# A fused Mamba and RWKV layer: the residual by accumulating transposes, a norm's factor on VectorE, another order of the stages

## What is computed

```python
x = x + mamba(layernorm(x))          # ends in its own norm over y @ W_out + its input
x = x + rwkv_channel_mix(layernorm(x))

# mamba(xn), D = 256 channels, N = 16 states
x, z = split(xn @ W_in)
delta = softplus((x @ W_x)[:, :D] @ W_dt + b_dt)
B, C  = the other 2 * 16 columns of x @ W_x
h_t   = exp(delta_t * A) * h_(t-1) + delta_t * x_t * B_t     # for each channel and state
y_t   = sum over the 16 states of h_t * C_t, + x_t * D_param
res   = (y * silu(z)) @ W_out + xn
out   = norm(res) * ln_g + ln_b

# rwkv_channel_mix(h): r = sigmoid(mix_r @ W_r.T); k = relu(mix_k @ W_k.T) ** 2; out = r * (k @ W_v.T)
```

## Time and profile before

| | |
|---|---|
| three runs | 1000.49, 996.27 and 998.63 us, median 998.63 |
| the profiled execution | 995.58 us, span 993.7 us |
| PE, DVE, ACT, POOL busy | 94%, 92%, 92%, 94% of the span |
| mean granted clock | 0.983 of full speed |
| instructions of POOL on 128x1024 | 255 of dbx (L519), 144 of the C product (L532) |
| HBM | 164 GB/s over the span |

### The profile page before, as it was taken

How to read it: one execution, slowest core, us unless ns; L and a number is a source line. 1 busy time by engine, 2 the same in 40 slices (tenths; PEclk the granted TensorE clock), 3 DMA queues, 4 the chain that set the end, 5 groups by cost and what they waited for, 6 DMA issues and landing times.

```text
span 993.7 us, 15849 instructions
## 1 busy us (share of the span) xinstructions
PE 934.1 (94%) x5040; PEld 720.7 (73%) x5040; DVE 913.4 (92%) x1005; ACT 912.2 (92%) x2154; POOL 932.8 (94%) x409
## 2 busy tenths in 40 slices
PE   8757779999999999999999999999999999999997
PEld 5345566877868687786868778686877878688876
DVE  2899998999999999999999999999999999999875
...
GB/s 209 166 164 178 151 212 192 149 192 165 201 150 210 214 149 193 163 198 153 203 222 146 198 152 205 158 195 215 147 208 142 202 170 192 189 146 206 119 75 22
DMA packets 51473, 171.99 MB, mean 173 GB/s; under 512 B 5440, under 2 KB 32576, under 8 KB 35008
## 3 DMA queue, kind: packets, MB, share of 16 engines
...
...
HBM read 153.67 MB, written 9.44 MB: 164 GB/s over the span
## 4 chain that ended last, share of the span: by engine, by line
PE 45%; ACT 36%; DVE 8%; issue 7%; POOL 2%; DMA 1%; SPq 0%; DVEq 0%; ACTq 0%; POOLq 0%
PE w_ps L1249 12%; ACT da_ps L632 11%; PE y_ps L1233 10%; PE w_ps L1242 9%; DVE da_ps L986 3%; ACT xn_tok L572 3%; DVE hg L986 3%; PE w_ps L1314 2%; ACT spare L578 2%; PE w_ps L1371 2%; PE w_ps L1355 2%; ACT L782 2%; ACT L773 2%; ACT zs L773 1%; ACT r_out L779 1%
## 5 line engine op out<-in xcount | busy, mean ns | idle before, releaser
L519 POOL TENSOR_TENSOR dbx<-u,b_ring 128x1024 f32<-128x1024 f32 x255 | 606.7, 2423 | 5.1 <-DVE da_ps L986 2.9
L632 ACT ACTIVATE da_ps<-delta,a_neg 128x512 f32<-128x512 f32 x512 | 334.2, 687 | 23.2 <-DVE carry L996 9.1
L532 POOL TENSOR_TENSOR hg<-hg,c_ring 128x1024 f32<-128x1024 f32 x144 | 349.3, 2426 | 0.5 <-ACT carry L638 0.5
L986 DVE TENSOR_TENSOR_SCAN hg<-da_ps,carry,dbx 128x512 f32<-128x512 f32 x218 | 265.7, 1266 | 11.3 <-ACT da_ps L632 9.2
L1233 PEld LDWEIGHTS y_ps<-ident,hg 128*128 128x128 f32 x2048 | 236.4, 142 | 49.7 <-issue 36.2
L1233 PE MATMUL y_ps<-ident,hg 128*128 128x128 f32 x2048 | 256.6, 275 | 9.9 <-POOL hg L532 6.6
L986 DVE TENSOR_TENSOR_SCAN da_ps<-da_ps,carry,dbx 128x512 f32<-128x512 f32 x166 | 205.0, 1275 | 3.5 <-ACT da_ps L632 2.4
L993 DVE TENSOR_TENSOR hg<-da_ps,c_ring 128x1024 f32<-128x1024 f32 x111 | 136.0, 1225 | 12.1 <-DVE da_ps L986 0.5
L986 DVE TENSOR_TENSOR_SCAN hg<-da_ps,dbx 128x512 f32<-128x512 f32 x72 | 83.8, 1207 | 4.4 <-ACT da_ps L632 4.4
L986 DVE TENSOR_TENSOR_SCAN da_ps<-da_ps,dbx 128x512 f32<-128x512 f32 x56 | 66.8, 1217 | 3.7 <-ACT da_ps L632 3.3
L1258 PE MATMUL w_ps<-w_rT,mixed 128*128 128x256 f32 x240 | 63.0, 385 | 7.1 <-DVE mixed L1036 7.1
...
## 6 DMA issues: line engine op xcount, KB each, us to landing
...
xres<-in_L_attn_x_in_dram SPq DMA_DIRECT2D x16, 512.0 KB, 4.7
x_tok<-in_L_attn_x_in_dram SPq DMA_DIRECT2D x15, 512.0 KB, 5.9
res<-xn_tok SPq DMA_DIRECT2D x15, 512.0 KB, 6.7
out_dram<-r_out SPq DMA_DIRECT2D x15, 512.0 KB, 3.2
...
```

Of the source, the lines that this page charges most:

```text
L519: pool.tensor_tensor(dbx[:, n % X_RING, :, :], u[:, ip, :, :], b.to_broadcast([P, KH, LC]), ALU.mult).then_inc(s["dbx_done"], 1)
L532: pool.tensor_tensor(part, part, c_of(n).to_broadcast([P, KH, LC]), ALU.mult).then_inc(s["g_pool"], 1)
L632: act.activation(da_of(n, h), delta[:, ip, h, :], ACT.Exp, scale=a_neg[:, h, n:n + 1]).then_inc(s["da_ready"], 1)
L986: dve.tensor_tensor_scan(out, da_of(n, h), dbx[:, n % X_RING, h, :], 0.0 if first else carry[:, n, h:h + 1], ALU.mult, ALU.add).then_inc(s ...
```

## The change

Five edits.

1. xnT, the normalised chunk in channel order, becomes a ring of three (XN_RING). The residual is made from it: four transposing matmuls of 128x128 a half (`residual`) that open the bank in place of two matmuls of 128x256. The buffer res, its DMA, its semaphore and the second buffer of xn_tok go.
2. nr is made by one TENSOR_TENSOR of 128x4 on DVE (`scaled_mean`), at the new stages nr1 and nr3 of VEC_TURN, nr1 of VEC_HEAD and nr3 of VEC_TAIL; the four ACT instructions go.
3. All tables of stages and of banks are new.
4. LAST_SPLIT is [2, 3, 8, 14]: of the last chunk, the C products of columns 5 and 6 move from DVE to POOL.
5. The closing part's residual uses the same function.

```diff
+XN_RING = 3
-LAST_SPLIT = [2, 3, 5, 6, 8, 14]
+LAST_SPLIT = [2, 3, 8, 14]
-VEC_TURN = dict(mix0=3, mix1=3, gate=4, sp0=5, u0=6, x20=10, x21=10, sp1=12, u1=13, v0=13, v1=14)
+VEC_TURN = dict(mix0=3, mix1=3, gate=4, sp0=5, u0=6, x20=10, x21=10, sp1=11, u1=12, v0=12, nr3=13, v1=14, nr1=15)
-               wo1=5, wo0=5, dt1=7, xa0=7, xa1=7, z0=8, z1=8, v0=9, la1=9, v1=12, xo0=12, xo1=14, xD=14)
+               wo1=5, wo0=5, dt1=7, xa0=7, xa1=8, z0=9, la1=9, v0=10, z1=10, xo0=10, xD=10, v1=11, xo1=13)
...
-        xn_tok = sb("xn_tok", P, 2, TB, D)
-        xnT = sb("xnT", P, KH, LC)
+        xn_tok = sb("xn_tok", P, TB, D)
+        xnT_ring = sb("xnT", P, XN_RING, KH, LC)
...
-        res = sb("res", P, TB, D)
...
-                if scan and not late:
-
-                    if mid:
-                        for _, unit in last_uses(t, ["wo0", "wo1"]):
-                            need_ready(sp, t, unit)
-                    sp.dma_start(res[:, :, :], xn_tok[:, par, :, :]).then_inc(s["res_set"], 16)
...
-                if ln in nr:
-                    need(act, ln_rs[ln], count)
-                    for j in range(TB):
-                        last = act.activation(nr[ln][:, j:j + 1], nm[ln][:, j:j + 1], ACT.Copy, scale=rs[ln][:, j:j + 1])
-                    last.then_inc(ln_nr[ln], 1)
...
                         need(act, ln_nr[1], t + 1)
-                        need(act, s["res_set"], 16 * t)
...
-                            from_pre(f"xnT{m}", xnT[:, m, :])
+                            from_pre(f"xnT{m}", xnT_ring[:, (t + 1) % XN_RING, m, :])
...
+                def scaled_mean(ln, count):
+
+                    need(dve, ln_rs[ln], count)
+                    dve.tensor_tensor(nr[ln][:, :], nm[ln][:, :], rs[ln][:, :], ALU.mult).then_inc(ln_nr[ln], 1)
...
+                    if more and at("nr1"):
+                        scaled_mean(1, t + 3)
+                    if mid and at("nr3"):
+                        scaled_mean(3, t)
...
+            def residual(out, c, v):
+
+                for b in range(2):
+                    tokens = slice((2 * v + b) * P, (2 * v + b + 1) * P)
+                    for k in range(KH):
+                        pe.matmul(by_block(out)[:, b, k * P:(k + 1) * P], xnT_ring[:, c % XN_RING, k, tokens], ident[:, :],
+                                  is_transpose=True, start=b == 0 and k == 0, stop=False, skip_group_check=True)
...
-                        need(pe, s["res_set"], 16 * t)
-                        for b in range(2):
-                            pe.matmul(by_block(out)[:, b, :], ident[:, :], res[:, 2 * m + b, :], start=b == 0, stop=False,
-                                      skip_group_check=True)
+                        residual(out, t - 1, m)
```

More of the change, by code:

```diff
@@ L43 @@
+                sum31=12, sum3_set=12, sq3=12, rs3=12, z1=13, ev0=13, rs1=14, dl1=14, norm3=14, z_set=15, ev1=15)
+VEC_TURN = dict(mix0=3, mix1=3, gate=4, sp0=5, u0=6, x20=10, x21=10, sp1=11, u1=12, v0=12, nr3=13, v1=14, nr1=15)
 PE_TURN = dict(hT0=0, xnT0=0, xnT1=0, x0=1, x1=1, hT1=2, dt0=2, r1=2, r0=2, k0=3, bc=3, la0=3, gT0=4, gT1=4, k1=5,
-               wo1=5, wo0=5, dt1=7, xa0=7, xa1=7, z0=8, z1=8, v0=9, la1=9, v1=12, xo0=12, xo1=14, xD=14)
-BANK = dict(wo1=2, gT0=2, wo0=0, x0=2, k0=2, v0=2, x1=1, hT1=2, dt0=1, hT0=0, xnT0=2, k1=1, gT1=0, z1=0, v1=0, r0=2,
-            r1=0, xnT1=1, z0=2, bc=0, dt1=1)
@@ L50 @@
-ACT_HEAD = dict(xnT0=0, xnT1=0, consts=1, sum1=1, bc=1, dt0=1, ln0=1, dt1=2, ln1=4, x0=5, x1=5, z1=6, dl0=9, sq1=13,
-                dl1=13, z0=14, rs1=15, z_set=15)
-VEC_HEAD = dict(center=4, small=8, sp0=11, sp1=11, u0=11, u1=12, ffn=14)
-PE_HEAD = dict(xnT0=2, xnT1=2, bc=2, dt0=3, dt1=3, x0=4, x1=6, z1=11, la0=11, la1=11, z0=12, ffn=14)
-ACT_TAIL = dict(prev=0, hT0=1, hT1=1, silu=3, gT0=4, gT1=4, sq20=5, k1=6, sq21=6, rs2=6, late_prev=7, k0=7, square=7,
-                sum30=7, sum31=8, sum3_set=8, sq3=8, rs3=8, norm3=8, ev0=8, late_hT0=9, late_hT1=9, ev1=10,
-                late_k0=11, late_k1=12, late_square=12, late_silu=14, late_ev0=15, late_ev1=15)
@@ new lines @@
+BANK = dict(hT1=2, hT0=0, x1=1, k0=2, dt0=1, r0=0, gT1=2, wo0=0, v1=2, xnT0=2, x0=2, xnT1=1, v0=0, z1=2, gT0=0, wo1=2,
+            dt1=1, bc=0, z0=0, r1=2, k1=1)
+ACT_HEAD = dict(xnT0=0, xnT1=0, consts=2, sum1=2, bc=2, dt0=3, ln0=3, dt1=4, ln1=4, x1=6, x0=8, z0=9, dl0=11, sq1=12,
+                z1=12, rs1=14, dl1=14, z_set=14)
+VEC_HEAD = dict(small=0, center=3, sp0=4, sp1=8, u0=9, u1=12, ffn=14, nr1=14)
+PE_HEAD = dict(xnT0=0, xnT1=1, bc=2, dt0=3, dt1=3, x0=6, x1=7, z0=8, la0=12, la1=13, z1=14, ffn=14)
@@ new lines @@
+ACT_TAIL = dict(prev=0, hT0=1, hT1=1, silu=3, gT0=4, gT1=4, k0=5, sq20=5, sq21=6, rs2=6, k1=7, square=7, sum30=7,
+                sum31=8, sum3_set=8, sq3=8, rs3=8, norm3=8, ev0=8, late_prev=9, late_hT0=9, late_hT1=9, ev1=10,
+                late_k0=11, late_k1=12, late_square=12, late_silu=14, late_ev0=15, late_ev1=15)
+VEC_TAIL = dict(mix0=1, mix1=1, gate=2, x20=6, x21=6, nr3=8, v0=8, v1=8, late_mix0=9, late_mix1=9, late_v0=14,
+                late_v1=14)
+PE_TAIL = dict(hT0=0, hT1=1, r0=2, r1=2, gT0=3, gT1=3, k0=3, wo0=4, wo1=4, k1=5, xa0=6, xa1=6, xD=6, v0=7, v1=7,
+               xo0=7, late_hT0=8, late_hT1=9, xo1=9, late_k0=11, late_k1=11, late_r1=12, late_r0=13, late_v0=13,
+               late_v1=14, late_xo0=15, late_xo1=15)
@@ L729, in step @@
                         need(act, ln_nr[1], t + 1)
-                        need(act, s["res_set"], 16 * t)
-                        norm(blocks_of(xn_tok[:, nxt, :, :]), blocks_of(x_tok), scalars_of(rs[1]),
+                        norm(blocks_of(xn_tok), blocks_of(x_tok), scalars_of(rs[1]),
                              scalars_of(nr[1]), s["xn_done"])
@@ L930, in first_norm @@
                 for j in range(TB):
[L931 removed]
+                    last = dve.tensor_scalar(xn_tok[:, j, :], x_tok[:, j, :], first_mean[:, j, 0:1], rs[1][:, j:j + 1],
                                              ALU.subtract, ALU.mult)
@@ L1288, in pre_unit @@
                         need(pe, s["xn_done"], i + 1)
-                        last = turned(out, xn_tok[:, nxt, :, :], m)
+                        last = turned(out, xn_tok, m)
                     elif unit in ("x0", "x1"):
@@ L1405, in gated_turned @@
                     turn_half(GT_LAST[v], gated_tok, v).then_inc(last_turned[v], 1)
-                def residual(v):
-                    for b in range(2):
-                        pe.matmul(by_block(WO_LAST[v])[:, b, :], ident[:, :], xn_tok[:, LAST % 2, 2 * v + b, :], start=b == 0,
-                                  stop=False, skip_group_check=True)
                 def wo(v):
@@ L1441, in close @@
                 need(pe, s["g_vec"], splits(LAST, NS - 1))
-                residual(0)
+                residual(WO_LAST[0], LAST, 0)
                 for n in range(NS - Y_LAG, NS - 1):
@@ L1449, in close @@
                 wo(0)
-                residual(1)
+                residual(WO_LAST[1], LAST, 1)
                 wo(1)
```

15 lines of the change are left out of this document (5 added, 10 removed).

## The result

| | before | after |
|---|---|---|
| median | 998.3 us (4 runs) | 1018.04 us (4 runs, 1012.37 to 1020.84) |
| ratio | | 1.019, 95% interval 1.014 to 1.024 |
| profiled execution | 995.58 us | 1020.84 us, span 1019.0 |
| PE, DVE, ACT, POOL busy | 94, 92, 92, 94% | 91, 92, 88, 92% |
| mean granted clock | 0.983 | 0.973 |

The account below looks back on a forecast made before the run. POOL was taken as the bound, 25 instructions or 58.0 us a step. Middle -1.0, head -0.3 and last step -0.6 made -1.9 us, from a median of 998.63 to 996.7 us; range 993 to 1006.

Parts of the forecast that it names:

- The small factor, DVE's side: New 128x4 products on DVE: at most 0.15 us each, 0.3 a step, covered by 1.7 us idle time; 0.
- Rival 1: The new DVE product waits for POOL's instruction under way, 2.3 us a step: 1006 us, worst 1039; chance 0.20.
- The argument against the rival: Middle steps: a DVE waiting for POOL's end is set to POOL's beat, so its next wait is just idle time.
- L1153's 0.15 us: DVE's last product: 0.84 us against 0.69 with one PSUM input; a wait for POOL or the form's cost.
- The small factor, ACT's side: Four ACT instructions gone for each norm, 1.7 us a step off ACT, hidden by POOL's work: 0.
- The residual: PE's transposes save 0.42 us a half, 0.84 a step, on an engine with 1.0 us idle: 0 in the middle.
- The order in the middle: u1 comes before column 13's scans, so POOL's waits for it end: -1.0 us, bounds -1.3 and 0.
- The head: Before the middle steps: POOL's 0.5 us wait behind the first carry can go; -0.3 us.
- The last step: POOL gets 4.64 us more work but its 4.2 us of waits go: -0.6 us, bounds +1.0 and -1.3.
- POOL's pitch: One POOL instruction every 2.32 us, 25 a step; another pitch would show the forecast wrong.
- rival 3: Faster: all waits go (-3.1 us) and POOL's pitch falls 0.01 us over 400 instructions: 991.5 us; chance 0.14.

Follow-up runs that it names:

- e17: The kernel before, with the residual by transposes, the change's four-column list and its tables for the last step; nr stays on ACT: 995.71 us, 0.9986.
- e3: The changed kernel, with nr made on DVE by four products of 128x1 instead of one of 128x4: 1000.09 us, 1.0024.
- e12b: The kernel before, with an unneeded DVE product of two 128x4 tensors behind every column, 256 in all: 1198.3 us, one execution.
- e2: The kernel before, with two unneeded DVE products of two 128x4 tensors a step, behind columns 13 and 15: 1016.12 us, 1.0188.
- e4: The kernel before, with the residual by transposes alone (edits 1 and 5 of the change): 995.07 us, 0.9972.
- e1: The changed kernel, with nr made by ACT's four instructions again, all else of the change kept: 1011.64 us, 1.0146.
- e14: e1 with ACT's sq3 moved from column 12 to 13 and rs3, with nr's four instructions, from 12 to 14: 1056.7 us, 1.0597.
- e9: The kernel before, with two extra DVE sums over 128x4 a step, behind columns 13 and 15: 998.34 us, 0.9989.
- e16: e4 with the change's tables for the last step and before's list of six DVE columns: 995.51 us, 0.9985.

## Why the prediction was wrong

The parts, from the ratios and a before of 998 us: the residual alone 0.997 and 0.9972, about -3 us; the last step's list and tables on top (e17, 0.9986) +1.5, hardly more than the scatter; the other tables, with nr off ACT in a form that does not wait (e3, 1.0024) +4; the form that waits (1.019 and 1.0216) +17 to +19. Together +20.

- **The small factor, DVE's side: 0 forecast, 17 to 19 measured.** This is the step that failed. The forecast took 0.15 us from a copy that reads PSUM and asked only whether 1.7 us of idle time cover 0.3. The duration without POOL was right (0.13); what it waits for is not in that row.
- **Rival 1 named the mechanism and had the wrong size.** It took "each waits 0 to 2.32 us, 1.16 in the mean" and priced it by DVE's idle time at 1006; the 1018 lies between that and its worst, 1039. For 255 of 256 in e12b the bound of one POOL instruction holds. But the price lay in the exceptions, 10.1, 6.3 and 6.9 us, which run over several. The argument against the rival, that DVE is set to POOL's beat, was right in the middle of the change: its steps 4 to 14 take 58.02 to 58.56, those of e3, which has no such wait, 57.98 to 58.71. It left out what it costs to get onto the beat, and that the last step has another; in e2's order it does not hold at all. The sentence of the Trainium skill, SBUF — State Buffer, § Who interferes with whom, on the two-port modes, "Whoever issues first gets the shared pair for the whole instruction", gives a wait of one instruction at most; at 88.74 the trace shows over four, and the trace decides.
- **L1153's 0.15 us was a wait.** The prediction left open whether the form itself costs it. The last product of 128x512 on DVE, both inputs in SBUF, stands in all 19 traces. It takes 0.68 or 0.69 us where POOL's own last product has at most 0.14 us left, as in the change, and ends 0.55 us behind POOL's end where it has 0.29 to 0.62 left: 0.84 to 0.88 and 1.14 to 1.17 us. The two products in e3, where POOL ends at 970.18:

```profile
968.89 1.29 POOL L551 TENSOR_TENSOR hg<-hg,c_ring 128x512 f32<-128x512 f32 x1
...
969.57 1.16 DVE L1153 TENSOR_TENSOR hg<-hg,c_ring 128x512 f32<-128x512 f32 x1
```

- **The small factor, ACT's side: 0 forecast.** True for before's order, where e4, with nr on ACT, runs at POOL's 58.0. Not for the change's: from e3 to e1 it is 11.5 us. That ACT has 1.2 to 1.7 us of idle time says nothing about a new order. Which place in it is the cause is open, since e14 moved the wrong one.
- **The residual: 0 forecast, -2 to -3 measured.** The saving of 0.42 us a half was read rightly: the groups take 0.93 us in the mean before and 0.51 in e4. PE's idle time of 1.0 us was taken for cover. In e4 the step is flat and POOL's waits for u1 are gone, 0.7 us in before's trace; the sum of the steps falls by 1.3 and what is behind them by 0.5. The rest is not located. That it is PE's 0.84 us a step that brings u1 forward, and not the DMA or norm1's freed wait, was not tested apart; PE's busy time over the span falls by 3.8 us only (934.1 to 930.3), not by 15 x 0.84.
- **The order in the middle: -1.0 forecast, about +4 with the head.** The waits for u1 do end, but the residual alone does that too. In their place POOL waits 2.6 us, 12 times, for the scans of columns 13 and 15 (e3). "The same 0.1 us could be lost at another stage" stood in the text with the bound 0; it could be a loss.
- **The head: -0.3 forecast.** Nothing in it: POOL began at 27.26 before and at 27.33 and 27.37 in e3 and e4, which have the new and the old head. The wait of 0.5 that was to go is 2.2 in e3 and e4, and in e9 with before's own head, and 0.5 in e16: it goes with the clock of the eight matmuls shown above.
- **The last step: -0.6 forecast, +0.6 to +1.4 measured without the wait** (e17 against e4). The working held: POOL's waits of 4.2 us go, and its last product, forecast to end at 965.4, ends at 965.9 in e17 and 965.0 in e4; the gain on PE did not reach the end. With the wait it is 8 us.
- **POOL's pitch** stayed at 2.32 us, and rival 3 with it.
